# First layer of a graph network: biases folded into the weight products, empty columns from a bfloat16 diagonal, node features in eight parts

## The reference

```python
def _layer(h, M, W_in, b_in, W_out, b_out, W_self, b_self, gamma, beta):
    A = M / (jnp.sum(M, axis=0, keepdims=True) + EPS)
    mask = A > THRESH
    W = jnp.where(mask, A, 0.0)
    T = h @ W_in + b_in
    weighted_sum = jnp.einsum('ji,jd->id', W, T)
    weight_sum = jnp.sum(W, axis=0)
    has_edge = jnp.any(mask, axis=0)
    agg = jnp.where(has_edge[:, None], weighted_sum / (weight_sum[:, None] + EPS), T)
    agg = agg @ W_out + b_out
    out = agg + (h @ W_self + b_self)
    ...   # layer norm over the features, gamma, beta
```

## Time and profile before

| what | value |
|---|---|
| median of 3 timed runs | 1056.03 us |
| the profiled execution's own time | 1051.33 us |
| its span | 1049.6 us |
| mean granted TensorE clock over the span | 0.989 |
| TensorE busy | 1002.7 us, 96% |
| VectorE busy | 424.1 us, 40% |
| ScalarE busy | 312.9 us, 30% |
| GpSimd busy | 177.0 us, 17% |
| first layer, from the first product to the last piece of block 7 | 8.2 to 356.4 us |

### The profile page before, as it was taken

How to read it: one execution, slowest core, us unless ns; L and a number is a source line. 1 busy time by engine, 2 the same in 40 slices (tenths; PEclk the granted TensorE clock), 3 DMA queues, 4 the chain that set the end, 5 groups by cost and what they waited for, 6 DMA issues and landing times.

```text
span 1049.6 us, 12440 instructions
## 1 busy us (share of the span) xinstructions
PE 1002.7 (96%) x3614; PEld 530.9 (51%) x3614; DVE 424.1 (40%) x1460; ACT 312.9 (30%) x595; POOL 177.0 (17%) x207
## 2 busy tenths in 40 slices
PE   6999999999999999999999899779999999999997
PEld 3545545545555544444444488634445454454444
DVE  4333233232333244444343255661433534534365
ACT  4256455456452100000000145322213223122231
POOL 3100100100100111222212135451010110100101
PEclk8999999999999999999999999979999999999999
DMA  9965862662601498887772844147554564645300
GB/s 374 401 265 202 357 275 99 269 259 96 287 1 41 190 369 303 316 319 295 305 287 79 315 134 129 46 138 273 209 200 189 215 250 161 241 181 203 129 8 14
DMA packets 40916, 221.03 MB, mean 211 GB/s; under 512 B 6530, under 2 KB 22724, under 8 KB 28930
## 3 DMA queue, kind: packets, MB, share of 16 engines
q1 hardware_dynamic: 37698, 215.60, 53.7%
q0 software_dynamic: 2864, 4.39, 1.2%
q10 hardware_dynamic: 272, 0.13, 0.0%
HBM read 210.68 MB, written 11.62 MB: 212 GB/s over the span
## 4 chain that ended last, share of the span: by engine, by line
PE 78%; DVE 6%; ACT 5%; issue 4%; DMA 2%; DVEq 2%; POOL 1%; POOLq 1%; SPq 0%; ACTq 0%
PE PA L1742 20%; PE PA L1527 20%; PE PA L1547 15%; PE O L1719 3%; ACT U L666 3%; PE O L1785 3%; PE O L1596 3%; PE T L1805 2%; PE T L1794 1%; PE SR L1785 1%; PE SM L1785 1%; DMA S<-in_x_cols 1%; PE O L1764 1%; PE O L1558 1%; ACT work L612 1%
## 5 line engine op out<-in xcount | busy, mean ns | idle before, releaser
L1547 PE MATMUL PA<-ring,S 128*128 128x512 f32 x512 | 231.0, 599 | 7.9 <-DVE S L883 7.9
L1742 PE MATMUL PA<-ring,S 128*128 128x512 f32 x512 | 233.4, 596 | 2.0 <-ACT S L681 2.0
L1527 PE MATMUL PA<-ring,U 128*128 128x512 f32 x512 | 226.4, 595 | 0.0
L1547 PEld LDWEIGHTS PA<-ring,S 128*128 128x128 f32 x512 | 96.7, 192 | 115.4 <-issue 104.3
L1527 PEld LDWEIGHTS PA<-ring,U 128*128 128x128 f32 x512 | 94.8, 190 | 107.2 <-issue 107.1
L1742 PEld LDWEIGHTS PA<-ring,S 128*128 128x128 f32 x512 | 92.1, 190 | 100.4 <-issue 96.5
L591 ACT ACTIVATE work<-ring 128x2048 int8<-128x2048 f32 x64 | 122.2, 1910 | 8.9 <-DMA ring<-in_adj_cols 4.2
L1403 DVE TENSOR_TENSOR U<-ring,work 128x512 f32<-128x512 f32 x112 | 81.5, 730 | 88.4 <-PE SR L1785 44.7
L719 ACT ACTIVATE work<-T,work 128x64 f32<-128x64 f32 x112 | 29.1, 311 | 66.7 <-PE T L1794 54.2
L811 POOL DMA_INDIRECT disp_d<-work x32 | 32.0, 999 | 96.0 <-DVE work L1249 88.7
L823 POOL DMA_INDIRECT y_d<-R,work x40 | 39.0, 974 | 54.1 <-DVE R L1319 44.4
(11 more groups left out here) (243 smaller groups left out, 1066.3 us busy)
## 6 DMA issues: line engine op xcount, KB each, us to landing
ring<-in_adj_cols SPq DMA_DIRECT2D x55, 2048.0 KB, 8.8
ring<-in_adjT_cols SPq DMA_DIRECT2D x32, 2048.0 KB, 7.6
work<-in_w SPq DMA_DIRECT2D x16, 256.0 KB, 3.0
ring<-in_Wr SPq DMA_DIRECT2D x1, 4096.0 KB, 12.2
ring<-in_Wr SPq DMA_DIRECT2D x2, 2048.0 KB, 13.6
disp_d<-U SPq DMA_DIRECT2D x4, 650.0 KB, 19.6
work<-disp_d SPq DMA_DIRECT2D x8, 325.0 KB, 4.0
ring<-in_adj_cols SPq DMA_DIRECT2D x2, 1024.0 KB, 7.9
```

Of the source, the lines that this page charges most:

```text
L1527: mm = nc.tensor.matmul(out_T[:, :], X[:, t * D:(t + 1) * D], ring[slot][t // HT][:, (t % HT) * BW:(t % HT + 1) * BW], start=n == 0, stop= ...
L1547: mm = nc.tensor.matmul(PA[k % 2][:, :], S[:, t * D:(t + 1) * D], ring[slot][t // HT][:, (t % HT) * BW:(t % HT + 1) * BW], start=t == 0, s ...
L1742: mm = nc.tensor.matmul(PA[slot][:, :], S[:, t * D:(t + 1) * D], ring[1][t // HT][:, (t % HT) * BW:(t % HT + 1) * BW], start=t == 0, stop= ...
```

## The change

- The bias of the input product becomes column 127 of the difference matrix (`t_in1d`), so that W_io carries it in its row 127, which meets the column sums in aT. The two remaining biases become row 127 of W_s1 by a product over two partitions (`at_last`, `t_b1`). `bias_rows`, `b_io`, `b_all` and the scales `cc` go; `self_rows` on VectorE becomes a copy.
- The spread row of sums (L1516) and ScalarE's `empty_cols` go. VectorE marks empty tokens from the per-token sums (`nn`), multiplies a bfloat16 identity with them into a 128x512 tile `empties`, and TensorE spreads it with a bfloat16 product of `onesb` and `empties` into SR, as a new piece `empty_cols` at place 5. VectorE waits for it (`s_erow`) before the branch and multiplies SR with the own features.
- The code behind the branch is written shorter.
- `x` arrives in 8 parts of 4 tiles. VectorE works on them in pairs: moments of two parts, then normalising the same two.
- `turn_z`, `layer2_products` and `self_rows` stand one place earlier, `turn_h` of step 0 one later.

```diff
-XPARTS = ((0, 4), (4, 8), (8, 16), (16, 24), (24, 32))
+XPARTS = tuple((t, t + BT) for t in range(0, NT, BT))
...
             load_x(2)
+            load_x(3)
             load_first(1, s_ring[slot_of(0)][0])
-            load_quarter(sp, adjc, blk(0), slot_of(0), 1)
-            load_x(3)
-            load_quarter(sp, adjc, blk(0), slot_of(0), 2)
-            load_x(4)
-            load_quarter(sp, adjc, blk(0), slot_of(0), 3)
+            for q in range(1, 4):
+                load_quarter(sp, adjc, blk(0), slot_of(0), q)
+                if q < 3:
+                    load_x(2 * q + 2)
+                    load_x(2 * q + 3)
...
-                if c > 0:
-                    normalise_x(c - 1)
-            normalise_x(XC - 1)
+            for c in range(0, XC, 2):
+                for some in (moments_x, normalise_x):
+                    some(c)
+                    some(c + 1)
...
-            def empty_cols(k):
-                if blk(k) == FREE - 1:
-                    act.wait_ge(s_fill, FILLED)
-                act.wait_ge(s_srow, k + 1)
-                alone(act)
-                nc.scalar.activation(U[:, cols_of(k)], SR[:, :], ACT.Relu, bias=ones[:, 0:1], scale=EMPTY_SCALE).then_inc(s_ind, 1)
...
                 nc.vector.tensor_scalar(sumc, SM[:, 0:BT], EPS, None, ALU.add)
+                nc.vector.tensor_scalar(nn, SM[:, 0:BT], 0.0, None, ALU.is_le)
...
                 nc.vector.scalar_tensor_tensor(bad, smax, SUM_MAX, bad1, ALU.is_ge, ALU.add).then_inc(s_bad, 1)
+                nc.vector.tensor_tensor(tiles(empties), identb.unsqueeze(1).to_broadcast([P, BT, P]), nn.unsqueeze(2).to_broadcast([P, BT, P]),
+                                        ALU.mult).then_inc(s_diag, 1)
...
                 dve.wait_ge(s_flag, k + 1)
                 alone(dve)
+                dve.wait_ge(s_erow, k + 1)
+                alone(dve)
...
-                nc.vector.tensor_tensor(ws_, ws_, rw_, ALU.mult)
-                nc.vector.tensor_tensor(cc[slot], ws_, ne[:, tb], ALU.add)
...
-                    nc.vector.tensor_tensor(tiles(z1[:, some], 2, DH), tiles(O[u][:, :], 2, DH), b_all[:, :].unsqueeze(1).to_broadcast([P, 2, DH]),
-                                            ALU.add).then_inc(s_zpre, 1)
+                    nc.vector.tensor_copy(z1[:, some], O[u][:, :]).then_inc(s_zpre, 1)
...
-            def bias_rows(k):
-                for t in range(BT):
-                    zt = z1[:, t * DH:(t + 1) * DH]
-                    nc.vector.scalar_tensor_tensor(zt, b_io[:, :], cc[k % 2][:, t:t + 1], zt, ALU.mult, ALU.add)
-                dve.drain()
...
-                dve.wait_ge(s_ind, k + 1)
-                alone(dve)
                 dve.wait_ge(s_hT, k + 1)
                 alone(dve)
-                nc.vector.tensor_tensor(U[:, cols_of(k)], U[:, cols_of(k)], hT[k % 2], ALU.mult)
-                dve.drain()
-                nc.vector.tensor_tensor(aT, aT, U[:, cols_of(k)], ALU.add).then_inc(s_aT, 1)
+                nc.vector.tensor_tensor(pA, SR[:, :], hT[k % 2], ALU.mult)
+                dve.drain()
+                nc.vector.tensor_tensor(aT, aT, pA, ALU.add).then_inc(s_aT, 1)
...
-                nc.tensor.matmul(SR[:, 0:DH], minus, t_s1, start=True, stop=True)
+                nc.tensor.matmul(SR[:, 0:DH], minus, t_s1, start=True, stop=False)
+                nc.tensor.matmul(SR[:, 0:DH], at_last, t_b1, start=False, stop=True)
...
-                for kk in range(KH):
-                    nc.tensor.matmul(O[0][:, DH:2 * DH], t_bin1[:, kk * P:(kk + 1) * P], t_out1[:, kk * DH:(kk + 1) * DH], start=kk == 0, stop=kk == KH - 1)
...
-                if k > 0:
-                    pe.wait_ge(s_ind, k)
-                else:
-                    pe.wait_ge(s_wready, 1)
-                nc.tensor.matmul(SR[:, :], sel, aT, start=True, stop=True).then_inc(s_srow, 1)
+
+            def empty_cols(k):
+
+                pe.wait_ge(s_diag, k + 1)
+                nc.tensor.matmul(SR[:, :], onesb[:, :], empties, start=True, stop=True).then_inc(s_erow, 1)
...
-            L1_PIECES = ((2, turn_h, 0), (2, column_sums, 1), (4, sum_verdict, 1), (9, out_rows, 1), (20, turn_z, 1),
-                         (23, layer2_products, 1), (29, self_rows, 0))
-            FIRST_PIECES = ((28, turn_h, 0), (30, lambda k: weight_products(), 0))
+            L1_PIECES = ((2, turn_h, 0), (2, column_sums, 1), (4, sum_verdict, 1), (5, empty_cols, 1), (9, out_rows, 1), (19, turn_z, 1),
+                         (22, layer2_products, 1), (28, self_rows, 0))
+            FIRST_PIECES = ((29, turn_h, 0), (30, lambda k: weight_products(), 0))
```

More of the change, by code:

```diff
@@ L125, in build @@
         ms, nm = [small[:, 64 + 4 * i:68 + 4 * i] for i in range(2)]
-        rbp, cc = [[small[:, 72 + 8 * i + 4 * j:76 + 8 * i + 4 * j] for i in range(2)] for j in range(2)]
+        rbp = [small[:, 72 + 4 * i:76 + 4 * i] for i in range(2)]
         smax, cdiff, bad1, bad = [small[:, 28 + i:29 + i] for i in range(4)]
@@ L884, in normalise_x, with moments_x @@
                 last.then_inc(s_hn, 1)
-            for c, (lo, hi) in enumerate(XPARTS):
+            def moments_x(c):
+                lo, hi = XPARTS[c]
                 dve.wait_ge(s_xin[c], 16)
@@ L933, in masked_sums @@
                 dve.drain()
-                nc.vector.tensor_tensor(pA, pA, X, ALU.add)
+                nc.vector.tensor_reduce(pA[:, 0:16], fix_turn.rearrange("p (b j) -> p b j", b=16, j=32), AX.X, ALU.add)
                 dve.drain()
-                nc.vector.transpose(X, pA)
+                for r in range(1, 4):
+                    nc.vector.tensor_copy(pA[0:32, 16 * r:16 * r + 16], pA[32 * r:32 * r + 32, 0:16])
                 dve.drain()
-                nc.vector.tensor_reduce(pA[:, 0:16], X.rearrange("p (b j) -> p b j", b=16, j=32), AX.X, ALU.add)
+                nc.vector.tensor_reduce(tot, pA[0:32, 0:64].rearrange("p (r b) -> p b r", r=4, b=16), AX.X, ALU.add)
@@ L948, in masked_sums, with masked_products @@
-                dve.drain()
+                nc.vector.transpose(fix_acc[0:32, :], fix_turn[0:32, :])
+                dve.drain()
+                for r in range(1, 4):
+                    nc.vector.tensor_copy(fix_acc[32 * r:32 * r + 32, :], fix_acc[0:32, :])
+                dve.drain()
+            def masked_products(k):
+                nc.vector.tensor_scalar(fix_acc, aT, sel, None, ALU.mult)
+                dve.drain()
+                row_of_sums(fix_acc)
+                nc.vector.tensor_scalar(thr, fix_acc, EPS, THRESH, ALU.add, ALU.mult)
+                dve.drain()
+                mask_block(slot_of(k), thr, pA)
+                nc.vector.memset(aT, 0.0)
+                with dve.Fori(0, D) as d:
+                    nc.vector.memset(fix_acc, 0.0)
+                    dve.drain()
+                    for h in range(2):
+                        with dve.Fori(0, HT) as t:
+                            nc.vector.scalar_tensor_tensor(fix_acc, ring[slot_of(k)][h][:, ds(t * BW, BW)],
+                                                           S[:, ds(t * D + d + h * HT * D, 1)], fix_acc, ALU.mult, ALU.add)
+                            dve.drain()
+                    row_of_sums(fix_acc)
+                    nc.vector.scalar_tensor_tensor(aT, fix_acc, ident[:, ds(d, 1)], aT, ALU.mult, ALU.add)
+                    dve.drain()
+                nc.vector.tensor_scalar(SR[:, :], fix_acc, 0.0, None, ALU.is_le)
@@ L949, in masked_sums @@
                 for c in range(4):
                     nc.vector.tensor_copy(ms[32 * c:32 * c + 32, :], tot.rearrange("p (t c) -> p c t", t=BT, c=4)[:, c, :])
-                nc.vector.tensor_copy(X[0:32, :].rearrange("p (b j) -> p b j", b=16, j=32), tot.unsqueeze(2).to_broadcast([32, 16, 32]))
-                dve.drain()
-                nc.vector.transpose(pA[0:32, :], X[0:32, :])
-                dve.drain()
-                for c in range(4):
-                    nc.vector.tensor_scalar(X[32 * c:32 * c + 32, :], pA[0:32, :], 0.0, None, ALU.is_le)
@@ L1123, in tail @@
                 dve.drain()
-                bias_rows(k)
                 out_tiles(k)
@@ L1617, in _ @@
             for k in range(1, NB):
-                step(k, L1_PIECES if k > 1 else L1_PIECES[:3] + ((6, self_rows, 1),) + L1_PIECES[3:])
+                step(k, L1_PIECES if k > 1 else L1_PIECES[:4] + ((6, self_rows, 1),) + L1_PIECES[4:])
             def tail_a(k):
```

111 lines of the change are left out of this document (32 added, 79 removed).

## The result

| | kernel before | changed kernel |
|---|---|---|
| median, same session (4 runs each) | 1056.28 us (1055.58 to 1057.64) | 1033.17 us (1031.92 to 1034.45) |
| profiled execution: own time, span | 1051.33, 1049.6 us | 1033.88, 1032.2 us |
| ratio of the times | 1 | 0.978 (0.9763 to 0.9797) |

The change takes 23.1 us away, 22.5 were forecast. The two profiled executions differ by 17.4 us only. So the stages are compared by the starts of their instructions. Counted from the span's start, the first transposes of the second layer begin at 366.03 us before and at 341.62 after: 24.4 us in the first layer.

A forecast was written before the change was run, and what follows sets the result against it. TensorE, 96% busy, was taken as the bound, so only its work and waits count. Terms -8.0 - 5.6 - 0.45 - 7.4 - 1.8 = -23.2, rounded to -22.5, gave 1033.5 us from 1056.0; range 1028.5 to 1046.5.

The forecast's parts named there:

- the quarters: Step 0: the matrix lands in quarters; tiles 8 to 15 were to start at 17.1 us, when quarter 1 lands.
- drains that might stay: Whole sum: part of the drains may stay, so -23.2 us was rounded to -22.5.
- Start, -8.0: Step 0: x in smaller pieces lets TensorE's tiles begin earlier; -8.0 us, bounds -3 and -8.5.
- TensorE's row, -5.6: Each of eight blocks: spread row in bfloat16, 0.25 us for float32's 0.95; -5.6 us, bounds -2.8 and -5.9.
- Weight products, -0.45: Folded weights: two 256-column bias products go, one over two partitions comes; net -0.45 us.
- `out_rows`, -7.4: TensorE's waits at out_rows: shorter jump cuts the branch gap to 1.64 us; -7.4 us, bounds +1.2 and -8.5.
- `turn_z`, -1.8: TensorE's wait at turn_z: normalised rows come about 2.0 us earlier without bias rows, so the wait goes; -1.8 us.
- Steps 1 to 8 together, -14.8: The forecast terms for the eight blocks: TensorE's row -5.6, out_rows -7.4 and turn_z -1.8 us.
- The first rival, 1046: Branch in each block: gap stays near 3.8 us in six blocks, saving only 9.9 us, or 1046; chance 18%.

The follow-up runs named there:

- the repeat: The changed kernel, unchanged, run again beside the kernel before on the third session's chip: 1032.05 us, ratio 0.9777.
- e4_fp32_row: The changed kernel with the row of empty columns spread in float32 in place of bfloat16: 1037.16 us, ratio 0.981.
- e10_erow_late: The changed kernel with VectorE's wait for the row of empties moved from ahead of the cast to behind the branch: 1029.68 us, ratio 0.9744.
- e6_bias_time: The changed kernel with four VectorE operations of the old bias rows' form, adding zero, put in front of the outputs: 1033.36 us, ratio 0.9825.
- e11_old_places: The changed kernel with turn_z, layer2_products and self_rows back at places 20, 23 and 29: 1032.32 us, ratio 0.9773.
- e2_short_branch: The kernel before without the masked-column products behind the branch, 55 or 56 instructions jumped in place of 243 or 244: 1043.16 us, ratio 0.9867.
- e1_start_only: The kernel before with only the start changed: x in eight parts, worked on in pairs, turn_h one place later: 1056.7 us, ratio 0.9994.
- e3_long_branch: The changed kernel with 130 never-run memsets added behind the branch, 222 or 223 instructions jumped in place of 92 or 93: 1057.61 us, ratio 1.000.
- e7_longer_branch: The changed kernel with 250 never-run memsets behind the branch, 342 or 343 instructions jumped, one run: 1058.79 us.
- e8_before_again: The kernel before, unchanged, run and profiled once more on the chip of the second session: 1051.71 us.

## Why the prediction was right, point by point

The time was right and so was the mechanism: the start is held by the quarters, and the shorter code behind the branch takes away the waits at `out_rows`. Some of the closeness is luck. The sum was -23.2 and was rounded to -22.5 for drains that might stay; no run shows such a remainder. The first layer gave 24.4 us between the profiles, the medians 23.1 and, in the repeat, 24.5. By its own steps:

- **Start, -8.0.** `turn_h` begins at 35.62, behind one more product than before; at the old place it would be 34.76, 7.7 us before the 42.49 of the earlier trace rows. The gap ahead of tile 8 did not lower the clock. Right, 0.3 too large.
- **TensorE's row, -5.6.** 0.22 us of queue where 0.25 was taken; putting the float32 row back costs 5.1 (`e4_fp32_row`). Right.
- **Weight products, -0.45.** Wrong. From `weight_products` to the next product it takes 39.70 - 36.92 = 2.78 us; before, by the starts 44.65 and 47.48 in the same view, 2.83. The two bias products of before (L1497, below) did give back 46.81 - 45.94 = 0.87. The product over two partitions holds the queue for 38.07 - 37.44 = 0.63 us, where about 0.45 was taken; that is no less than the product over 128 partitions ahead of it (0.52). Its neighbours take 0.09 and 0.11 more than before.

```profile
45.94 1.03 PE L1497 MATMUL O<-R 128*128 128x256 f32 x4
46.81 0.61 PE L1499 MATMUL O<-R 128*128 128x128 f32 x4
```

- **`out_rows`, -7.4.** The waits fell by 7.6. The gap is 1.11 to 1.81 where 1.64 was taken. The prediction left 8 x 0.1 for the chain and 0.3 for block 0's self rows; the view of waits has 0.9 for block 0, and `e10_erow_late` shows some 0.1 in four other blocks. So the new wait ahead of the cast is just at the edge: in five blocks aT is what `out_rows` starts on. Right.
- **`turn_z`, -1.8.** The wait went, and the rows were ready 0.57 us early where 0.7 was reckoned. In the kernel as built the bias rows' removal was needed for it: the same time put back brings a wait in every block (`e6_bias_time`), and without the bias rows the earlier place neither costs nor gains (`e11_old_places`). What the prediction missed is that the short branch alone removes this wait too, with the bias rows and the old places both present (`e2_short_branch`). The 1.8 us can't be put down to one of the two.
- **Steps 1 to 8 together, -14.8.** Measured -16.6. Three experiments come to the same by another way: -12.95 for the short branch and -5.1 for the row, and 1.6 given back by the row's wait, make -16.45. The 1.8 us over the forecast fit what a wait costs beyond its recorded idle time, 12.95 against 10.3 in `e2_short_branch`; the prediction took each wait at its idle time.
- **The first rival, 1046.** Priced wrongly. When the branch stays long the time is 1057.6, equal to before: the rival counted the waits and neither the fall of the granted clock behind them nor block 0's fetch behind full DMA queues (1.0 to 1.7 us over the 4.16 that it has without).
- **Additivity.** The sum treats its terms as independent. The start alone brings nothing (`e1_start_only`, ratio 0.9994), since with a long branch it moves block 0's branch into full DMA queues, and a seventh gap is long there; taken out of the changed kernel it costs 0.65% or 6.9 us (0.9845 against 0.978, from two sessions). The terms could be added only because the branch was short.

The Trainium skill (Runtime: NRT & Kernel Launch, Instruction fetch mechanics) has blocks of 256 instructions; for VectorE here, `e3_long_branch` and `e7_longer_branch` contradict its size and agree with its rule that a target outside the resident blocks is fetched.

## What to carry to other kernels

Look at the idle time behind a taken branch on an engine that another one waits for: if it is long in some iterations and short in others, cut the code that is jumped over, or branch earlier. Such code costs time without running once the jump is long enough, and more when the branch falls where the DMA engines are full. Where two engines run this close, look at how far behind its releaser an instruction starts: a view of waits can show none. Do not price a wait by its idle time alone where the granted clock falls behind it, and do not judge one part of a change by itself where another part decides what its gain meets.

## What the runs showed of the hardware that was not expected

- Queue 14, taken for VectorE's instruction queue, moves 8 KB packets (0.38 MB in 46). A taken branch that needs one shows a gap of 3.7 to 4.3 us, one that does not 1.1 to 1.9 with the load of the register in it. In block 0 of the three kernels with the new start and a long branch, where the gap begins with the DMA engines full (share 1.02 in `e1_start_only`), it lasted 5.2 to 6.8.
- A float32 product of 256 columns over two partitions is no cheaper than one over 128: 0.63 us against 0.52.
- After waits of 2.4 and 4.98 us the granted clock of TensorE was 0.50 in the next windows (1.2 GHz), after those of 1.50 and 1.15 us TensorE kept its pace; after one of 1.90 it was 0.55. The length of the wait alone does not settle it: behind block 0's wait for the self rows, 2.33 us in one profile of the kernel before and 2.35 in the other (`e8_before_again`), it was 1.00 and 0.50. What else it depends on was not tried.
- The expert stage, from its first transposes to the products behind the last store, took 89.8 to 90.0 us in the four profiles of the second session and in that of before, and 94.4 to 96.05 in all others, with variants of both kernels on both sides. In the longer ones TensorE waits for ScalarE; these are the changed kernel's waits there:

```profile
PE PA L1463 <- DMA y_d<-R,work: 11.7, 1, 11.7
PE PA L1667 <- ACT U L658: 2.4, 5, 0.5
```

The first row is 10.6 in the profile of before, and the second is absent from the shorter ones. It goes with the session, or in the profile of before with the execution, and not with the kernel; its cause stays open.
